# Four-layer kernel, third attention: where the last output projections stand in TensorE's order

## The reference

```
q = (x @ wq).reshape(b, s, H, HD)        # H = 16 heads of HD = 128
k = (x @ wk).reshape(b, s, KV, HD)       # KV = 4
v = (x @ wv).reshape(b, s, KV, HD)
q, k = apply_rope(q, cos, sin), apply_rope(k, cos, sin)
scores = where(causal, q @ k.T / sqrt(HD), min)
probs = softmax(scores, axis=-1)
out = (probs @ v).reshape(b, s, H * HD)
return out @ wo                          # the output projection
h = hidden_states + attn_out
out = h + moe(rmsnorm(h, norm2_w), ...)  # a mixture of experts follows
```

## Time and profile before

| | us |
|---|---|
| median of 3 runs (lowest, highest) | 1499.85 (1498.85, 1501.99) |
| the profiled execution's own time | 1488.37 |
| its span in the trace | 1486.6 |
| TensorE matmul busy (share of the span) | 1303.5 (88%) |
| VectorE busy | 1048.2 (71%) |
| ScalarE busy | 720.4 (48%) |

### The profile page before, as it was taken

One profiled execution on the slowest core, in us unless ns is written; L12 is line 12 of the kernel. 1 busy time (PEld: TensorE's weight loads), 2 busy tenths in 40 slices (PEclk: granted clock), 3 DMA queues, 4 the chain that ended last, 5 costly groups with the idle time before them and its releaser, 6 DMA issues.

```text
span 1486.6 us, 20851 instructions
## 1 busy us (share of the span) xinstructions
PE 1303.5 (88%) x6620; PEld 906.9 (61%) x6620; DVE 1048.2 (71%) x2211; ACT 720.4 (48%) x1836; POOL 216.2 (15%) x227
## 2 busy tenths in 40 slices
PE   8688869986998668999998689985999999889998
PEld 4344445552333244677676589974888888764555
DVE  7999987888896787777877623225666666668565
ACT  5788823443775665555544112223666666633111
POOL 0132220000000002222220173111111111201000
PEclk9899979995999869999999799997999999989999
DMA  5122240015330200000004198845222222101230
GB/s 189 71 99 99 86 191 1 1 28 87 65 59 6 78 1 1 1 37 1 36 1 134 43 345 309 301 176 180 94 71 71 71 71 71 35 1 47 77 91 29
DMA packets 77776, 124.61 MB, mean 84 GB/s; under 512 B 44965, under 2 KB 56430, under 8 KB 72352
## 3 DMA queue, kind: packets, MB, share of 16 engines
q1 hardware_dynamic: 75824, 119.37, 24.8%
q0 software_dynamic: 1872, 4.22, 0.7%
HBM read 88.28 MB, written 26.24 MB: 77 GB/s over the span
## 4 chain that ended last, share of the span: by engine, by line
PE 66%; DVE 18%; issue 7%; ACT 4%; DMA 3%; POOL 1%; SPq 1%; DVEq 1%; ACTq 0%; POOLq 0%
DVE roomA L753 5%; PE psum L3181 5%; PE psum L2397 5%; PE psum L1978 4%; PE psum L2687 4%; PE psum L2739 4%; PE psum L873 4%; PE psum L2717 4%; PE psum L2020 3%; PE psum L2765 3%; PE psum L3191 3%; PE psum L2408 2%; PE psum L2010 2%; PE psum L1374 2%; DVE roomB L1535 2%
## 5 line engine op out<-in xcount | busy, mean ns | idle before, releaser
L2804 ACT ACTIVATE roomA<-psum,roomA 128x256 f32<-128x256 f32 x128 | 70.9, 559 | 92.7 <-DVE roomA L2870 92.4
L2066 ACT ACTIVATE roomA<-psum,roomA 128x128 f32<-128x128 f32 (+1 forms) x128 | 53.2, 426 | 88.4 <-DVE roomA L2141 88.2
L1535 DVE TENSOR_REDUCE roomB<-psum 128x2 f32<-128x512 f32 x128 | 82.1, 686 | 10.8 <-PE psum L1374 9.3
L2539 DVE SCALAR_TENSOR_TENSOR roomA<-roomA,psum 128x512 f32<-128x512 f32 x23 | 15.9, 690 | 101.7 <-ACT roomA L2444 101.7
L1978 PE MATMUL psum<-own,roomB 128*128 128x512 f32 x160 | 75.0, 594 | 3.4 <-DVE roomA L2133 2.1
L1941 POOL TENSOR_TENSOR roomA<-roomA 128x512 f32<-128x512 f32 x40 | 51.0, 1275 | 176.8 <-DVE roomA L2134 176.8
L3181 PE MATMUL psum<-roomA,roomB 128*112 128x512 f32 (+1 forms) x168 | 74.8, 593 | 0.3 <-DVE roomA L3409 0.3
L2739 PE MATMUL psum<-roomA 128*128 128x256 f32 x256 | 68.3, 389 | 6.0 <-DVE roomA L2882 4.4
L753 DVE TENSOR_TENSOR_SCAN roomA<-roomA 128x1024 f32<-128x1024 f32 x32 | 73.1, 2284 | 0.0
L1374 PE MATMUL psum<-roomB,roomA 48*128 48x256 bf16 x256 | 53.0, 308 | 16.2 <-DVE roomB L1535 8.7
L2717 PE MATMUL psum<-roomA 128*128 128x256 f32 x256 | 65.6, 379 | 1.7 <-ACT roomA L2804 1.7
(11 more groups left out here) (526 smaller groups left out, 3328.0 us busy)
## 6 DMA issues: line engine op xcount, KB each, us to landing
roomB<-m_w_dram SPq DMA_DIRECT2D x12, 1536.0 KB
roomA<-m_w_dram SPq DMA_DIRECT2D x11, 1536.0 KB
a_kv_ready<-roomB SPq DMA_DIRECT2D x32, 512.0 KB, 3.1
roomA<-a_kv_ready SPq DMA_DIRECT2D x8, 1024.0 KB, 4.8
roomA<-a_kv_ready SPq DMA_DIRECT2D x16, 512.0 KB, 4.3
roomB<-a_w_dram SPq DMA_DIRECT2D x4, 1280.0 KB, 5.9
roomB<-f_w_dram SPq DMA_DIRECT2D x8, 624.0 KB, 3.9
roomA<-f_c_rows SPq DMA_DIRECT2D x6, 512.0 KB, 3.9
```

Source lines behind the costliest of these rows:

```text
L1535: dve.tensor_reduce(maxneg[:, hp // 8, :, m, hp % 8], g.bank(m).rearrange("p (q k) -> p q k", k=S), AX.X, ALU.max, negate=True).then_inc(s ...
```

## The change

From step 28 on, where no projection of q, k or v is left, the two halves of an output projection stand in different steps, each between the transposes (`turn`) and the product with V (`weigh`). The turn of step 27 keeps its first half where it was, at the end of step 27, and its second half goes into step 28. The turn of step 29 goes into steps 29 and 30, that of step 31 into steps 31 and 32. The last turn (n = 15) stands whole behind the loop, as before. Steps 0 to 26 issue the same instructions in the same order. The number of instructions and the waits by value are the same; the waits for `a3_ot` and `a3_added` go with the first half, the signal `a3_out` with the second.

```diff
+    LAST_JOB = PAIRS - 5
...
-        def out(n):
+        def out(n, r):
             wo = parts(n // B % 2)[3]
-            pe.wait_ge(s["a3_ot"], 2 * n + 2)
-            if n:
-                pe.wait_ge(s["a3_added"], n)
-            for r in range(2):
-                for h in range(HQ):
-                    ins = pe.matmul(g.bank(OUT)[:, r * D:(r + 1) * D], OT[:, n % 2, h, r * P:(r + 1) * P], wo[:, h, :],
-                                    start=(h == 0), stop=(h == HQ - 1))
-            ins.then_inc(s["a3_out"], 1)
+            if r == 0:
+                pe.wait_ge(s["a3_ot"], 2 * n + 2)
+                if n:
+                    pe.wait_ge(s["a3_added"], n)
+            for h in range(HQ):
+                ins = pe.matmul(g.bank(OUT)[:, r * D:(r + 1) * D], OT[:, n % 2, h, r * P:(r + 1) * P], wo[:, h, :],
+                                start=(h == 0), stop=(h == HQ - 1))
+            if r:
+                ins.then_inc(s["a3_out"], 1)
...
+            if t > LAST_JOB and t % 2 == 0:
+                out(out_in(t - 1), 1)
+            elif LAST_JOB < t < PAIRS:
+                out(out_in(t), 0)
             if 1 <= t <= PAIRS:
                 weigh(t - 1)
             for f, what in jobs[1:]:
                 project(f, what)
-            if out_in(t) is not None:
-                out(out_in(t))
+            if out_in(t) is not None and t <= LAST_JOB:
+                out(out_in(t), 0)
+                if t < LAST_JOB:
+                    out(out_in(t), 1)
+        for r in range(2):
+            out(TURNS - 1, r)
```

## The result

The changed kernel takes 1486.12 us (median of 7 runs, 1482.89 to 1491.86); the kernel before took 1496.17 in the same comparison (7 runs, 1492.87 to 1501.99, the three shown ahead among them). The ratio is 0.9931, 95% interval 0.9908 to 0.9954: 10 us faster, between 7 and 14. The forecast was 1493.3 in a range from 1490.5 to 1497.5, so the measured time lies outside, on the fast side. One execution of the kernel before took 4553 us, where all others took 1488 to 1505; it is left out of every figure.

A forecast was written before the change was run, and what follows sets the result against it. TensorE was taken to bound the stage, with five holes of 7.1 us behind ScalarE's copy. Holes and weight loads saved 8.0, lateness and step 32's start returned 1.5: 1499.85 - 6.5 = 1493.3 us, range 1490.5 to 1497.5.

The forecast's parts named there:

- What bounds the stage: Steps 27 to 33: TensorE sets the pace, with five idle holes, 7.1 us together, ended by ScalarE's copy of the transposes.
- The sum by steps: From `weigh(26)` to `weigh(31)`: 1.73 + 5.05 + 5.70 + 5.05 + 5.70 + 3.95 = 27.2 us instead of 33.7.
- The lateness term: VectorE reaches the scores of steps 29 and 31 0.66 us late, after `add` waited for a half.
- rival (a): VectorE is punctual after all in the stage: gain 8.0 less 0.2 to 0.3, time 1492.1; chance 0.13.
- First in, first out on VectorE: Normalisations stay behind the waiting `add`, gain 6.5; let past, 8.0 less the start of step 32; no row showed it.
- The moved wait: First halves of turns 13 and 14 wait for `keep` and `add` in front of `weigh`; hidden with 0.5 us reserve.
- Rival (b): First half before `weigh` waits for `keep`, stopping TensorE's queue: gain about 4 us, time 1495.8; chance 0.18.
- Behind the stage: After the last `keep`, everything moves along with it; the last projection stays beside the normalisation.
- Rival (c): Something with a fixed time behind the stage holds, or halves don't hide: under 3 us gained, about 1499; chance 0.09.
- Rival (d): Clock comes back late behind the stage, first expert blocks at 1.2 GHz: 1504 with two such blocks; chance 0.04.
- The profiled execution against the median: Gain summed on an execution of 1488.37, carried unscaled to the median of the runs shown: 1499.85 - 6.5 = 1493.3.

## Why the prediction was right and where it failed

*What bounds the stage* was right: the holes were the copy's, and the product with V starts without one wherever a half fills it and VectorE is punctual.

*The sum by steps* was right within 0.2 us: 5.03 and 5.05 for 5.05, 5.62 and 5.63 for 5.70, 3.95 for 3.95, stretch 27.03 for 27.2. The lateness term was 0.57 per odd step instead of 0.66, and the hole that it leaves 0.40 instead of about 0.5. Moving the `add` removed it, so its cause is shown, and rival (a), VectorE punctual, fell.

*First in, first out on VectorE:* the row that was missing is there now, a reciprocal whose input was ready at 795.71 and which started at 797.40 behind the waiting `add`. The Trainium skill ("TensorE: Matmul & The Clock Gate", architectural detail of the array) says that VectorE's queue is strictly first in, first out; this trace agrees.

*The moved wait* of the first half never showed: in steps 29 and 31 the projection follows the transposes at once (799.34 + 0.66 = 800.00). Rival (b) fell.

*Behind the stage* was right as far as single traces tell: 662.9 and 662.8 us from the last `keep` to the end. That they agree to a tenth is luck: the second traces of the same two kernels had 666.3 and 669.1. Rival (c), a fixed time that holds, fell. Rival (d), the clock, did not decide. What it took is seen up to the scatter: 25.0 to 25.3 us instead of 24.4 to 24.8, all of it in the first logits. That the granted clock sets their length is shown by the idle matmuls.

*The step that failed is "The profiled execution against the median":* 1499.85 - 6.5. The gain was carried over rightly, the level was not. Over 94 executions the kernel before has a median of 1494.45, with single ones from 1487.75 to 1504.59; the three that I took as its level lay 5.4 above that. Of the other 91 only 5 reach the lowest of these three, so they are hardly a chance draw from the same scatter; what set them apart is not on record. From 1494.45 the same subtraction gives 1488.0, and the 36 executions of the changed kernel have 1487.35. The sign that I had and passed over: the profiled execution lay 11.5 us under the three runs, so single executions were known to differ by more than the whole gain. The range was too narrow for the same reason: it allowed 1.5 us of scatter on either side, from three runs that spanned 3.1. So of the 7.2 us between forecast and result 5.4 are the level and 0.6 the gain (7.1 between the two medians instead of 6.5). The remaining 1.2 us down to 1486.12 are within what seven executions with a deviation of 3.4 leave open.

What makes executions differ was not isolated. The repeats ran on three different chips, at different times. Mean granted clock and time go together (among the timed executions of the kernel before 1487.75 us came with 0.940 and 1500.14 with 0.929), and in the changed kernel's second trace the part from 343 to 461 us had a granted clock of 0.80, where the first trace had 0.86. Why the clock is granted differently from one execution to the next stays open.

## What to carry to other kernels

Here a wait between two steps of one engine was worth filling only at that place: the same halves of a projection gave 6.7 us between the transposes and the product that waits for their copy, and 2.5 us ahead of the transposes. After moving work on one engine, look at who waits for its end on the others: an `add` in front of two normalisations gave 1.2 of 7.9 us of the stretch back. And an absolute time forecast from three runs inherits their level; compare the profiled execution with them first and widen the range by that distance.

## What the runs showed of the hardware

Behind a pause on TensorE the same matmuls can take nearly twice as long. In the changed kernel, with 2.1 us of idle time in front of the normalisation's transposes, the granted clock fell from 2.4 to 1.2 GHz during the first sixteen matmuls of the logits; the two sixteens took 3.15 to 3.56 and 3.60 us instead of the 1.94 and 1.97 that they took at 2.4 GHz. With eight idle matmuls in that pause the fall came behind the first sixteen in two traces (1.94) and within them in a third, with the `add` moved (2.37). With four more ahead of each half both sixteens ran at 2.4 GHz, in one trace. Up to the scatter 23.0 and 21.4 us were left of 25.0; no time of a whole execution shows this gain. Whether the pause alone makes the clock fall, or the small matmuls behind it too, these runs don't separate.
